# Two stores, then two loads: regrouping GpSimd's transfers in a normalise-and-blur kernel

## What is computed

```python
def _gn(v, G=32, eps=1e-5):                      # 32 groups of 12 channels
    g = v.reshape(B_, G, C_ // G, H_, W_)
    m = jnp.mean(g, axis=(2, 3, 4), keepdims=True)
    s = jnp.var(g, axis=(2, 3, 4), keepdims=True)
    return ((g - m) / jnp.sqrt(s + eps)).reshape(v.shape)

def _L0_conv_ref(inp, offset):                   # 48 positions of 8 channels, K = 3, SIGMA = 0.5
    off_round = jax.lax.stop_gradient(jnp.round(offset))
    out = _displace(inp, off_round.astype(jnp.int32))   # whole-pixel shift per position, zeros outside
    frac = offset - off_round
    dx = field_x[None] + frac[:, None, None, 0]
    dy = field_y[None] + frac[:, None, None, 1]
    kern = jnp.exp(-(dx * dx + dy * dy) / (2.0 * SIGMA ** 2))
    kern = kern / jnp.sum(kern, axis=(1, 2), keepdims=True)
    return conv_general_dilated(out, kern, ..., feature_group_count=C)   # 3 x 3, per channel

x = x + _L0_conv_ref(_gn(x), L0_conv_offset)
```

## Time and profile before

| | us |
|---|---|
| median of three runs | 971.57 |
| lowest and highest of them | 970.53, 972.0 |
| the profiled execution, its own time | 970.2 |
| its span in the trace | 968.4 |
| DMA engines, share of the span | 99.3% (queue of GpSimd) |
| bytes moved, mean rate | 403.48 MB, 417 GB/s |
| VectorE busy | 870.7 (90%) |
| ScalarE busy | 714.2 (74%) |
| GpSimd busy | 337.3 (35%) |
| TensorE busy | 201.4 (21%) |

### The profile page before, as it was taken

The page is one execution under the profiler, slowest core; times in us unless marked ns, Lnnn a source line. Parts: engine busy times, 40 slices in busy tenths (PEclk is TensorE's granted clock), DMA queues, the critical chain, the costliest instruction groups (busy, mean ns, idle before and its releaser), DMA issues.

```text
span 968.4 us, 3636 instructions
## 1 busy us (share of the span) xinstructions
PE 201.4 (21%) x896; PEld 195.9 (20%) x896; DVE 870.7 (90%) x940; ACT 714.2 (74%) x412; POOL 337.3 (35%) x196
## 2 busy tenths in 40 slices
PE   0331312212122121222202212212122122211220
PEld 0331312212122121222202212212122122210220
DVE  5489899999999999899989999999999979669991
ACT  3898959777597777878677776877868787777640
POOL 4022452633524432232325354252623413124320
DMA  8999999999999999999999999999999999999997
GB/s 354 425 408 427 423 418 420 420 422 415 397 430 420 400 428 429 422 417 430 418 425 418 419 408 430 416 415 418 406 432 415 427 428 430 423 427 425 410 432 336
DMA packets 28233, 403.48 MB, mean 417 GB/s; under 512 B 3506, under 2 KB 3506, under 8 KB 3634
## 3 DMA queue, kind: packets, MB, share of 16 engines
q0 software_dynamic: 27648, 402.67, 99.3%
q1 hardware_dynamic: 562, 0.57, 0.2%
HBM read 201.90 MB, written 201.33 MB: 416 GB/s over the span
## 4 chain that ended last, share of the span: by engine, by line
DVE 50%; DMA 35%; issue 5%; ACT 5%; POOL 3%; PE 0%; ACTq 0%; DVEq 0%; POOLq 0%
DMA out<-tiles,row_of 28%; DVE tiles L438 17%; DVE rowblur L413 9%; DVE tiles L440 9%; DVE rowblur L418 9%; DMA tiles<-x,row_of 7%; DVE normed L397 5%; ACT unread L243 4%; POOL tiles L184 2%; ACT unread L247 1%; DVE scale L352 0%; PE var_ps L217 0%; DVE shift L355 0%; DVE var_p L342 0%; DVE apart L336 0%
## 5 line engine op out<-in xcount | busy, mean ns | idle before, releaser
L243 ACT ACTIVATE unread<-tiles 128x4096 uint8<-128x4096 f32 x94 | 339.9, 3616 | 143.3 <-DMA tiles<-x,row_of 142.7
L247 ACT ACTIVATE unread<-tiles,nmean_p 128x4096 uint8<-128x4096 f32 x94 | 348.7, 3709 | 3.0
L184 POOL DMA_INDIRECT tiles<-x,row_of x96 | 162.0, 1687 | 488.7 <-DMA out<-tiles,row_of 483.6
L438 DVE SCALAR_TENSOR_TENSOR tiles<-rowblur,ratio,tiles 128x735 f32<-128x735 f32 (+24 forms) x192 | 300.0, 1562 | 4.6
L189 POOL DMA_INDIRECT out<-tiles,row_of x96 | 175.1, 1824 | 123.5 <-DVE tiles L438 101.0
L217 PE MATMUL mean_ps<-nmean_p,mask 128*128 128x1 f32 x448 | 100.7, 353 | 533.3 <-ACT unread L243 505.8
L217 PEld LDWEIGHTS mean_ps<-nmean_p,mask 128*128 128x128 f32 x448 | 98.0, 330 | 535.9 <-ACT unread L243 508.4
L413 DVE SCALAR_TENSOR_TENSOR rowblur<-normed,ratio 128x784 f32<-128x784 f32 (+14 forms) x96 | 152.3, 1586 | 3.4
L440 DVE TENSOR_TENSOR tiles<-rowblur,tiles 128x784 f32<-128x784 f32 (+14 forms) x96 | 146.5, 1526 | 3.3
L418 DVE SCALAR_TENSOR_TENSOR rowblur<-normed,ratio,rowblur 128x752 f32<-128x752 f32 (+14 forms) x96 | 145.4, 1515 | 3.4
L217 PE MATMUL var_ps<-var_p,mask 128*128 128x1 f32 x448 | 100.7, 353 | 199.3 <-DVE var_p L342 199.3
(11 more groups left out here) (34 smaller groups left out, 25.5 us busy)
## 6 DMA issues: line engine op xcount, KB each, us to landing
tiles<-x,row_of POOLq DMA_INDIRECT x96, 14.7
out<-tiles,row_of POOLq DMA_INDIRECT x96, 17.4
mask<-masks SPq DMA_DIRECT2D x1, 448.0 KB, 3.6
row_of<-rows SPq DMA_DIRECT2D x1, 48.0 KB, 1.7
offs<-offset SPq DMA_DIRECT2D x1, 48.0 KB
plan_sb<-planned SPq DMA_DIRECT2D x1, 0.4 KB
offs_p<-offset SPq DMA_DIRECT2D x1, 0.4 KB
steps_sb<-steps SPq DMA_DIRECT2D x1, 12.0 KB
```

Source lines behind the costliest of these rows:

```text
L184: pool.indirect_dma_start(tiles[:, n % SLOTS, :], None, x_rows, bass.IndirectOffsetOnAxis(ap=row_of[:, n:n + 1], axis=0)).then_inc(loaded[ ...
L243: nc.scalar.activation(unread[:], tiles[:, n % SLOTS, :], ACT.Identity, scale=-1.0 / HW, accum_out=nmean_p[:, i % 2, j:j + 1]).then_inc(nm ...
L247: nc.scalar.activation(unread[:], tiles[:, n % SLOTS, :], ACT.Square, bias=nmean_p[:, i % 2, j:j + 1], accum_out=m2_p[:, i % 2, j:j + 1]). ...
L438: ins = nc.vector.scalar_tensor_tensor(y, t, ratio[:, (tap + 1) // 2, p, 1:2], y, ALU.mult, ALU.add)
```

## The change

GpSimd's loop goes over pairs of tiles. It waits for tile n and issues its store, does the same for tile n + 1, and only then issues the two loads into the two slots, each behind the landing of its own store. The first ten loads and the waits at the end stay as they are, and no other engine's code is touched.

```diff
-            for n in range(ALL):
-
-                pool.wait_ge(col_taps, 1 + (n + 1) * COL_TAPS)
-                store(n)
-
-                if n and n - 1 + SLOTS < ALL:
-                    pool.wait_ge(stored[(n - 1) % SLOTS], landed(n - 1))
-                    load(n - 1 + SLOTS)
+            for pair in range(0, ALL, 2):
+                for n in (pair, pair + 1):
+
+                    pool.wait_ge(col_taps, 1 + (n + 1) * COL_TAPS)
+                    store(n)
+                for n in (pair, pair + 1):
+                    if n + SLOTS < ALL:
+
+                        pool.wait_ge(stored[n % SLOTS], landed(n))
+                        load(n + SLOTS)
```

## The result

| | before | after |
|---|---|---|
| median of the runs, us | 971.79 | 1054.24 |
| lowest and highest | 970.53, 975.91 | 1050.62, 1059.09 |
| ratio | | 1.0844, 95% interval 1.0812 to 1.0876 |
| span of the profiled execution | 968.4 | 1053.4 |
| GpSimd's DMA queue, share of the span | 99.3% | 96.5% |

What follows compares the result with a forecast made beforehand. The prediction took the DMA transfers, not VectorE, to bound the kernel. Its terms, 7 + 9 - 4 + 0 = +12 us on the profiled 970.2, made 982.2; with 1.4 us up to the median, 983.6 us, range 958 to 1004.

Steps and rivals of the forecast that it cites:

- disturbed stretches: Where loads and stores alternate, steps of a load and a store averaged 9.96 us against 9.73 undisturbed, 20 us in all.
- The thin spot: At the landing of a pair's second store only one load is left queued, 4.9 us instead of 9.7, about 43 times.
- Term 1: At each pair's second load the last engine runs dry when the issue takes over 2.2 us: +7 us, ends +5 and +19.
- the limits: Longest issue of a second load before an engine idles: 1.5 or 2.5 us by two traces, 2.2 taken.
- Term 2: The leading engine loses its 4.9 us lead, so disturbances cost what they cost the worst-hit engine: +9 us, between 0 and +20.
- Term 3: In the alternating stretch, half as many changes from store to load save time: -4 us, between 0 and -20.
- Term 4: Stores and loads that wait behind the new order still reach the queue in time: 0 us.
- A: From 61 to 908 us, mixing loads and stores was the disturbance, so grouping them is faster: 963.6 us, chance 0.23.
- B: At the loads, one transfer in the queue is enough and the costs and gains cancel: 971.6 us, chance 0.12.
- C: At the second loads, every issue over 1.5 us idles the engines: +39 us, near 1010 us, chance 0.17.
- The signs named for terms 1 and 2: DMA share 96 to 98%, below 0.9 after long second-load issues; end share falling within 2 us; pair steps over 20.1 us.

Runs made afterwards that it cites:

- the copy: Against the full kernels, nothing computed: GpSimd copies input to output in rounds of four loads and four stores, all waited for; loads first took 5.5 us more than stores first.

## Why the prediction was right in sign and wrong in size

**What bounds the kernel.** Right. The transfers bound both kernels, a transfer takes 4.87 us, and 20 us were lost before. That this loss came of "disturbed stretches" where loads and stores mix was wrong: it came at the loads, which went out with two transfers queued, and VectorE's long instructions made their issues late. The kernel by turns with a deeper queue ran at 431 GB/s, and short issues alone brought 14 us.

**The thin spot comes once a pair.** This is the step that failed first. The prediction counted the queue at the second store's landing (one load left) and not at the first's. When the first store lands, only the second store is queued, since the two loads behind it have not been issued: one transfer as well. There are two thin spots a pair, 86 and not 43, and both loads lose (1.10 and 1.45 us). The second step that failed is that a late load was priced by the time that engines stand idle and by nothing else: 54.9 of the 85.0 us are packets that took longer, for which the sum has no term.

**Term 1, +7 us.** Its fixed part was not too small. With nothing queued, landing, wake-up and start took 1.35 us, less than the 2.4 of the earlier trace rows and the 3.36 of the earlier trace rows, which the limits rest on. (The estimate of 0.7 us for landing and wake-up was good: 0.64.) What was wrong is the form: with one transfer queued there is no limit below which an issue is free. With all issues at 0.97 us the changed order still loses 61 us. Only 22 us answer to the length of issues, the one thing that term 1 priced.

**Term 2, +9 us.** The mechanism was seen and not its price. The engines did lose most of their lead (4.4 us to 2.0 us), and in the end the share falls later and faster than in the earlier trace rows:

```profile
1048.00:1050.00 2.00, 0.00 (x0) 0.00 (x0) 0.00 (x0) 0.00 (x0) 0.00 (x0) 1.00 0.99 426
1050.00:1052.00 2.00, 0.00 (x0) 0.00 (x0) 0.00 (x0) 0.00 (x0) 0.00 (x0) 1.00 0.54 229
1052.00:1053.40 1.40, 0.00 (x0) 0.00 (x0) 0.00 (x0) 0.00 (x0) 0.00 (x0) 1.00 0.00 0
```

But the loss is not, as term 2 had it, the old disturbance at its worst engine's price. Engines that have just run dry or nearly so are slow before the next turn: the load before it loses 1.39 us in the copy, and the second load of each pair 1.45, of which 1.12 are slow packets. These come to 48 us over the 43 pairs, and those of the first loads to 23, where the kernel before had 22 in all; no row of the kernel before that I looked at priced it.

**Term 3, -4 us.** Wrong. There was no gain to be had: with the queue deep enough (431 to 433 GB/s by turns), changing direction at each transfer costs nothing that shows.

**Term 4, 0.** Right: GpSimd waited for VectorE less than before, and the stores lost nothing.

**The rivals.** A fell with term 3. B fell. C was right that a thin spot bites at nearly every issue, but its price of 39 us was still less than half: it too counted one thin spot a pair and idle time alone. Its own objection, that the earlier trace rows are a cold start, was sound: there 1.86 us passed from the end of the issue to the first packet, and 0.71 in the kernel with nothing queued. The signs named for terms 1 and 2 came true (share 96.5%, no transfers left from 1052, steps of a pair above 20.1 us), but they don't vouch for the sum. The share fell as forecast although there were twice as many thin spots, and the steps were 22.04 us. That the thin queue would cost was right; what it costs was for the larger part something that the prediction did not have. The upper bound of term 1 had been halved by counting one thin spot, and no bound was set for slow transfers at all.

The Trainium skill, DMA: Bandwidth & Descriptors, gives about 2.0 us for the fixed part of one transfer, in its section on the anatomy of one DMA. Here landing, wake-up and start took 1.35 us, and with the shortest issue of 0.94 us 2.3, so the size agrees. By that figure the sum had come out lower still, since it holds nothing for the slow packets. That confirming the last byte is most of it is not what is seen here: the landing came 0.37 us after the last packet. The advice to issue early so that the fixed part is hidden, in its rules for kernel authors, is what the measurements bear out.

**What stays open.** Why the last packets before the first turn are slow once the engines have run dry. The copy shows it with nothing computed and all issues early, and that it shrinks when the stores are issued later. Whether it takes engines that are level, or only engines that have just stood empty, no run separates: in the copy both hold at the start of each round. Of the second load's 1.45 us, 1.12 are slow packets and the rest is idle time; that the slow ones are the copy's toll is argued from their place in the transfer, and not shown by a run that takes the turn alone away.

## What to carry to other kernels

Before regrouping transfers, write the queue out at each issue: what is still ahead when the instruction that issues comes back from its wait. Here one more store sent ahead was worth 81 us (1054.24 to 972.83), and different orders of the same 192 transfers ran from 966 to 1409 us. Depth that costs the computing engine its lead in the ring is lost again, so it is best added only where that engine is ahead.

## What the runs showed of the hardware

Four things I had not expected. An idle queue costs more than the gap: 5.4 us at each load, of which 2.0 are in a load that is already running, at 295 to 336 GB/s and full busy share. Right after the engines have stood empty, the transfer before the first change of direction is slow, by 1.4 to 1.7 us for a 2.1 MB load and 0.85 to 1.24 us for a store; the last packets of such a load, 16 KB each, take up to 1.18 us on average instead of 0.61. Later changes cost 0.1 to 0.6. An issue that GpSimd began while VectorE was inside a normalisation or a tap ended 0.85 us after the end of that instruction (median of 163), where an undisturbed one takes 0.96. And a busy share near 1 says nothing of the rate: between 110 and 1000 us the changed kernel shows a share of 0.97 at 381 GB/s, where the one before shows 1.00 to 1.01 at 417 to 421.
